# Reordering the vector engine's steps in the second half of a state-space mixer's turn (one NeuronCore)

## The reference

```python
xn = layernorm(x)                                   # 8192 tokens x 512 (4 sequences of 2048)
# mixer
x_input, x_gate = split(xn @ W_in.T)                # 1024 channels each
u  = silu(causal_conv4(x_input) + conv_b)           # depthwise, 4 taps
h  = scan(h = 0.95*h + 0.05*(u @ W_B.T))            # 64 states, along the sequence
y  = (h @ W_C.T + D_param*u) * silu(x_gate)
a  = layernorm(y @ W_out.T + xn) * ln_gamma + ln_beta
# 8 experts, each takes the 1024 tokens with the highest gate score
f  = xn; f[idx_e] += score_e * ffn_e(layernorm(xn[idx_e]))
out = x + a + f
```

## Time and profile before

| | us |
|---|---|
| median of 3 runs | 2916.48 |
| range of the 3 runs | 2914.75 to 2916.93 |
| the profiled execution | 2916.93 |
| its span, first to last instruction | 2915.2 |
| PE busy in the span | 2794.6 (96%) |
| DVE busy | 1849.0 (63%) |
| ACT busy | 1309.0 (45%) |
| POOL busy | 668.7 (23%) |

### The profile page before, as it was taken

The page is one execution under the profiler, slowest core; times in us unless marked ns, Lnnn a source line. Parts: engine busy times, 40 slices in busy tenths (PEclk is TensorE's granted clock), DMA queues, the critical chain, the costliest instruction groups (busy, mean ns, idle before and its releaser), DMA issues.

```text
span 2915.2 us, 40359 instructions
## 1 busy us (share of the span) xinstructions
PE 2794.6 (96%) x12424; PEld 2234.5 (77%) x12426; DVE 1849.0 (63%) x3098; ACT 1309.0 (45%) x2197; POOL 668.7 (23%) x909
## 2 busy tenths in 40 slices
PE   7789999999999999999799999999999999999997
PEld 3367888888887778888687878888788787887886
DVE  6457777777777788888755554555545554455553
ACT  3354444443343355555344444444444444444443
POOL 2243222222222222223311221012210111102211
PEclk9899999999999999999899999999999999999999
DMA  7742333333333333336314133041330413304121
GB/s 270 255 139 92 108 111 109 111 112 115 115 115 116 116 88 108 96 105 210 106 34 119 30 94 81 18 128 30 94 80 16 123 37 87 77 26 123 38 44 15
DMA packets 130326, 283.71 MB, mean 97 GB/s; under 512 B 14640, under 2 KB 14832, under 8 KB 130032
## 3 DMA queue, kind: packets, MB, share of 16 engines
q1 hardware_dynamic: 98096, 183.71, 19.4%
q0 software_dynamic: 32064, 97.85, 13.8%
HBM read 226.68 MB, written 54.82 MB: 97 GB/s over the span
## 4 chain that ended last, share of the span: by engine, by line
PE 47%; issue 2%; DMA 1%; DVE 1%; POOL 0%; ACT 0%; DVEq 0%; POOLq 0%; SPq 0%
PE po L1661 8%; PE po L1662 8%; PE po L1663 8%; PE ph L1661 8%; PE ph L1663 7%; PE ph L1662 7%; PE f_pt L1670 1%; DMA out_dram<-res,idx_c 1%; DMA rows<-xn_rows,idx_c 0%; POOL out_dram L1530 0%; DMA b<-b_in 0%; DVE res L1643 0%; DVE f_stats L504 0%; DVE hid_l L1621 0%; DVE w2l L1587 0%
## 5 line engine op out<-in xcount | busy, mean ns | idle before, releaser
L1661 PE MATMUL po<-w2h,hid_h 128*128 128x512 f32 x1024 | 405.6, 396 | 14.3 <-DVE hid_l L1621 14.3
L1299 PE MATMUL ring<-xt_h,w_h 128*128 128x512 f32 x1024 | 402.5, 393 | 10.6 <-ACT sg L1029 9.2
L1662 PE MATMUL po<-w2l,hid_h 128*128 128x512 f32 x1024 | 403.1, 394 | 0.0
L1301 PE MATMUL ring<-xt_h,w_l 128*128 128x512 f32 x1024 | 402.0, 393 | 0.0
L1663 PE MATMUL po<-w2h,hid_l 128*128 128x512 f32 x1024 | 401.7, 392 | 0.0
L1300 PE MATMUL ring<-xt_l,w_h 128*128 128x512 f32 x1024 | 400.0, 391 | 0.0
L1621 DVE TENSOR_TENSOR hid_l<-xn_tail,hid_h 128x512 fp32r<-128x512 f32 x256 | 175.5, 685 | 331.8 <-ACT hid_h L1578 326.2
L1119 DVE SCALAR_TENSOR_TENSOR u<-xin,cw,u 128x512 f32<-128x512 f32 x384 | 295.4, 769 | 118.2 <-ACT u L1011 97.4
L1574 ACT ACTIVATE xn_tail<-ph,b1c 128x512 f32<-128x512 f32 x256 | 176.2, 688 | 357.1 <-PE ph L1663 348.9
L1530 POOL DMA_INDIRECT out_dram<-res,idx_c x64 | 109.4, 1709 | 898.8 <-DVE res L1643 884.2
L1548 ACT CAST w1h<-w1r 128x512 fp32r<-128x512 f32 x258 | 160.3, 621 | 280.1 <-PE po L1663 268.5
(11 more groups left out here) (176 smaller groups left out, 5561.9 us busy)
## 6 DMA issues: line engine op xcount, KB each, us to landing
wo<-wo_halves POOLq DMA_DIRECT2D x120, 512.0 KB, 4.1
w1r<-fc_in SPq DMA_DIRECT2D x130, 256.0 KB, 2.7
w2r<-fc_in SPq DMA_DIRECT2D x130, 256.0 KB, 2.9
xn_rows<-g_ext SPq DMA_DIRECT2D x16, 1040.0 KB, 5.3
w1r<-x_in SPq DMA_DIRECT2D x16, 1024.0 KB, 7.8
rows<-xn_rows SPq DMA_DIRECT2D x16, 1024.0 KB, 6.5
xn_tail<-xn_rows SPq DMA_DIRECT2D x64, 256.0 KB, 2.6
x_tail<-x_in SPq DMA_DIRECT2D x64, 256.0 KB, 2.9
```

The lines of the kernel that those rows point to most:

```text
L1299: pe.matmul(ring[r % 2][:, :], w_h[:, r, q], xt_h[:, k, :], start=(k == 0), stop=False)
L1301: last = pe.matmul(ring[r % 2][:, :], w_l[:, r, q], xt_h[:, k, :], start=False, stop=(k == KD - 1))
L1661: pe.matmul(dst, ah, bh, start=start, stop=False)
L1662: pe.matmul(dst, ah, bl, start=False, stop=False)
```

## The change

In the second half of a turn, DVE's order within each step `c` is another. Before, `scale(c)` (or `finish(3)` at c = 4, or a `t_low` from c = 5 on) stood between `y_turn(c)` and `y_low(c)`, and `finish(c)` behind `y_low(c)`. Now `y_low(c)` and `side(c)` follow `y_turn(c)` directly, then come `scale(c)` and `finish(c)` one behind the other (c = 0 to 3), and the `t_low` of a quarter comes from c = 4 on at the end of the step. No instruction is added or removed, and the orders of the other engines are the same.

```diff
                     for c in range(NC_):
                         y_turn(b, c)
+                        y_low(b, c)
+                        side(c)
                         if with_end and c < J:
                             ends.scale(dve, b - 1, c)
-                        if with_end and c == J:
-                            ends.finish(dve, b - 1, J - 1)
-                        if 5 + lag <= c:
-                            t_low((b + 1) * KD + c - 5 - lag, c - 5 - lag)
-                        y_low(b, c)
-                        if with_end and c < J - 1:
                             ends.finish(dve, b - 1, c)
-                        side(c)
-                    for k in range(NC_ - 5 - lag, KD):
-                        t_low((b + 1) * KD + k, k)
+                        if c >= 4 + lag:
+                            t_low((b + 1) * KD + c - 4 - lag, c - 4 - lag)
+                    if lag:
+                        t_low((b + 1) * KD + KD - 1, KD - 1)
```

## The result

| | us |
|---|---|
| before, median of 4 | 2915.61 |
| after, median | 2993.18 |
| ratio after / before | 1.0264, 95% interval 1.0243 to 1.0284 |
| profiled execution of after | 2998.5 (span 2996.8) |

The change costs 77.6 us by the medians; 75.2 were forecast. The profiled execution of after took longer than the others that were compared (2990.17 to 2994.87); one more execution, slow at a granted clock of 0.55, took 10728.89 us and is left out of the comparison. In the changed kernel the lines behind the edit are three lower, so L1327 is the L1330 of before.

What follows compares the result with a forecast made beforehand. PE, busy 96% of the span, was taken as the bound, so its added waits count. Growth of 25.5 + 38.7 + 4.9 + 1.7 + 4.4 = 75.2 us on 2916.9 gave 2992 us, range 2978 to 3010.

Steps and rivals of the forecast that it cites:

- The place between `y_turn` and `y_low` is free, and what is taken out of it is paid: DVE, second half of a turn: work there costs nothing, moved work costs; `y_low(7)` pushed back 5.61 us, less DVE's waits.
- The pair: `scale` then `finish` of one tile on DVE behind `y_low`: 0.78 to the second start, then 0.66, together 1.44 us.
- the other value: The skill's rule that chaining costs nothing extra: 2 x 0.66 for `scale` and `finish`, ending at about 2986.5 us.
- Turns 1 to 8: Bisection turns: DVE's pushes less slack make each 3.19 us longer, 25.5 us together.
- the slack that I took off: DVE's spare time in turns 1 to 8: 2.10 us before `y_turn(3)`, 0.10 before `y_turn(7)`, 0.22 at `out_share(7)`.
- Turns 11 to 14: Token list turns: pushes plus waits for ACT's casts cost 10.2 us in turn 11, 9.5 in the others, 38.7 together.
- The stall: Turns 11 to 14: each of three `t_low`s waits 1.54 us for its cast, queued on ACT behind `numbers`.
- Turns 0, 9 and 10, 15: Growth of 1.7 us in turn 0, 4.9 in turns 9 and 10 together (estimated stall 0.6), 4.4 in turn 15.
- The clock: Rival, chance 0.18: PE's clock falls four to six times, about 3 us each, in turns 11 to 14; 3004 to 3010.
- the sum: All turns' growth added over the mixer: 75.2 us, giving 2992 us, chance 0.62.
- The sign that I had named for the clock: Mixer slices in the profile after showing PEclk under 9 would make the prediction wrong.
- Hidden, or faster: Rivals: pushes fit in DVE's waits, 2917, chance 0.04; `y_low` lets PE start earlier, up to 19.8 us, 2897, chance 0.03.

Runs made afterwards that it cites:

- `finish_between`: The changed kernel with `finish` one step later, between `y_turn` and `y_low`: 2974.00 us, ratio 1.0204 to before.
- the two halves: `ends_only` and `quarters_only`, each making one part of the change against the kernel before: 2953.94 and 2964.31 us.
- `cast_first`: The changed kernel with ACT's cast of a transposed quarter ahead of the same step's side work: 2979.87 us, ratio 1.0222 to before.
- `ends_only`: The kernel before with only `scale` and `finish` moved together behind `y_low` and `side`, `t_low` as before: 2953.94 us, ratio 1.0126.
- `filled`: The kernel before with `scale(3)` moved to step 2's end and later work put in its place before `y_low(3)`: 2905.39 us, ratio 0.9961.
- `quarters_only`: The kernel before with only the `t_low`s moved one step earlier, to the step's end, `scale` and `finish` as before: 2964.31 us, ratio 1.0158.

## Why the prediction was right, and where it was not

- *The place between `y_turn` and `y_low` is free, and what is taken out of it is paid.* Shown by the unchanged distance of 1.43 in after and `finish_between`, by 94.8 us of waits in after, and by the two halves.
- *The pair costs 0.78 + 0.66.* All 64 pairs of `scale` and `finish` in after stand 0.78 or 0.79 us apart, and 0.67 lie behind them, so the judged term held, and the other value, which would have given 2986.5, did not.
- *Turns 1 to 8: 3.2 each.* Undisturbed ones grew by 3.22 and 3.23; the slack that I took off (2.10 before `y_turn(3)`) was there: in after `y_turn(3)` came 0.22 late, forecast 0.24.
- *Turns 11 to 14: 10.2 and 9.5.* Turns 11, 13 and 14 grew by 10.18, 9.53 and 9.51. The stall was 1.46 by the view, 1.54 forecast, and `cast_first` took it away.
- *Turns 0, 9 and 10, 15.* Turn 0: 1.64 against 1.7. Turn 9: 2.69 against 2.4, as the stall was 0.95 and not the estimated 0.6. Turn 15: 2.29 against 4.4. It was 4.08 late at `out_share(4)`, where 3.78 was forecast, but gave back 2 us by `out_share(6)`. Before ran there at half clock for 6 us. After had its slow stretches a little earlier, and then the full clock. The windows of after:

```profile
1480.00:1486.00 6.00, 5.04 (x16) 3.82 (x16) 5.96 (x5) 0.00 (x0) 5.84 (x5) 0.72 0.35 113
1486.00:1493.00 7.00, 4.67 (x20) 3.24 (x20) 5.31 (x7) 2.18 (x4) 5.13 (x4) 1.00 0.00 0
```

  The other runs bear this out: from `out_share(4)` to `out_share(7)` of turn 15 `cast_first` and `finish_between` gave back 1.8 us too, `ends_only` 1.2 and `filled` 1.1, all with the slow stretch elsewhere or shorter. `quarters_only` had it where before had it, and gave back nothing (it lost 0.9):

```profile
1448.00:1456.00 8.00, 6.57 (x18) 5.26 (x19) 4.70 (x5) 1.73 (x4) 5.27 (x4) 0.57 0.00 0
```

- *The clock (a rival with 0.18).* It did fall, though not as I had it. I looked for falls only in turns 11 to 14 and at 3 us each. It fell in 13 of the 16 turns (all but 3, 6 and 9), mostly for some 3.4 us (the 0.76 over 7 us below), and in 10 of them around the 1.5 us of waiting at `out_share(4)`. Turns 4 and 6 of after have the same wait there, windows around `out_share(4)`:

```profile
549.00:556.00 7.00, 6.31 (x23) 5.11 (x24) 5.88 (x13) 1.52 (x3) 0.54 (x1) 0.76 0.28 99
...
711.00:718.00 7.00, 6.28 (x29) 5.20 (x30) 6.02 (x13) 1.56 (x3) 0.54 (x1) 1.00 0.51 152
```

  PEclk is 0.76 in the one and 1.00 in the other; in the first, there are 6 matmul records fewer. Turn 4 grew by 3.70, turn 6 by 3.22. `out_share(5)` came 1.5 us later in turn 4, but most of it vanished, since the next steps wait for DVE anyway.

  Only where DVE was not the bound behind a fall, or was itself held by PE, did it cost in full. Turn 12 grew by 11.11 against 9.53 in turn 13: its clock fell behind `out_share(7)`. The ends of both turns:

```profile
1228.00:1235.00 7.00, 6.75 (x23) 5.43 (x24) 1.39 (x3) 0.00 (x0) 0.53 (x1) 0.76 0.54 197
1318.00:1325.00 7.00, 6.20 (x27) 5.12 (x28) 1.89 (x3) 0.82 (x3) 0.53 (x1) 1.00 0.75 255
```

  Turn 10 grew by 4.18 against 2.69 in turn 9: its transposes came late, and DVE's wait for the cast of quarter 1 became 2.50 us in place of 0.95. In turns 0, 11, 13 and 14 a fall cost nothing.

  Added up against the undisturbed neighbours, the falls cost some 6.1 us in this execution, of which the sum had nothing: 3.0 in turns 1 to 8, 1.5 in turn 10, 1.6 in turn 12. So 75.2 + 6.1 - 2.1 (turn 15) + 0.5 (turns 9 and 10) + 0.3 (turns 1 to 8, 3.22 and not 3.19) makes the 80.0 of the turns. That the total came out so near is in part luck: two terms that the sum lacked, both of the clock, have opposite signs. The terms of DVE's order itself were right one by one, but for the stall of turns 9 and 10.

  The sign that I had named for the clock, slices with PEclk under 9, could not show it: a fall of 3.4 us lowers the mean of a slice of 75 us by 0.02, and the mixer's slices all read 9. Why the clock falls in turn 4 and not in turn 6, with the same wait, no run here settles. Nor was it shown what makes single executions of after differ by 8 us.
- *Hidden, or faster:* not seen. What PE lost in turns 0 to 14 it kept to the end: the turns account for 80.0 of the 81.6 us. That `y_low` can't come earlier than 1.43 us behind `y_turn` is what excluded a gain.
- One sign was forecast wrong: PE's waits for `y_low` were to reach 95 us, 75 us more than before. The view shows 58.3 and another 11.8 at `chan`, 47 us more; I had equated the view's idle time with the delay.

## What to carry to other kernels

Where an engine hands a value to another and takes the answer back, the time of the answer is a free place, here 1.43 us from start to start, of which some 0.8 can be filled. Putting the urgent consumer right behind its producer wins nothing while the answer is out, and it makes everything that stood between pay. Before moving an operation, measure the distance between producer and consumer where nothing stands between, and look at what the other engine has queued ahead of the value that the moved operation needs.

## What the runs showed of the hardware that was not expected

- PE's clock fell to its lower level in the middle of work after a wait of 1.57 us. The matmuls then started 0.43 us apart in place of 0.23, for some 3.1 us. The timeline of PE in after, turn 4:

```profile
549.69 0.79 PE L1327 MATMUL po<-wo,u_h 128*128 128x512 f32 x1 [1.57 <-DVE u_l L1154]
550.27 0.63 PE L1328 MATMUL po<-wo,u_h 128*128 128x512 f32 x1
...
551.13 0.63 PE L1327 MATMUL po<-wo,u_h 128*128 128x512 f32 x1
...
552.41 0.63 PE L1327 MATMUL po<-wo,u_h 128*128 128x512 f32 x1
552.83 0.44 PE L1328 MATMUL po<-wo,u_h 128*128 128x512 f32 x1
```

  and in turn 6, after the same wait, at the upper level:

```profile
711.72 0.49 PE L1327 MATMUL po<-wo,u_h 128*128 128x512 f32 x1 [1.57 <-DVE u_l L1154]
712.05 0.40 PE L1328 MATMUL po<-wo,u_h 128*128 128x512 f32 x1
```

  In before, the same place had a wait of 0.96 and no fall in turns 1 to 8. The wait alone does not decide it: of turns 1 to 8, all with a wait of 1.57 to 1.59 there, 6 had a fall in after, 5 in `cast_first`, 2 in `ends_only` and 2 in `finish_between`.
- A dependent pair of DVE operations (`scale` and `finish`) on 128x512 float32 in place costs 0.78 from start to start with its semaphore, an independent one 0.61 to 0.67.
